# A post-norm transformer layer on one core: in the last batch, who sums the softmax denominators and in which order the last norms, residuals and down products run

## The reference

```python
paths = sigmoid(x @ Wp + bp)                       # 8 heads x depth 5
agree = pq * pk + (1.0 - pq) * (1.0 - pk)
sim = cumprod(agree, axis=-1).sum(axis=-1) / DEPTH
sim = where(triu(k=1), -inf, sim); attn = softmax(sim)
ctx = attn @ (x @ Wv)
x = layernorm(x + ctx @ Wo)
h = silu(x @ wg.T) * (x @ wu.T)                    # hidden 768, int weights / 127
x = layernorm(x + h @ wd.T)
```

## Time and profile before

| | us |
|---|---|
| median of 3 runs | 849.27 (848.09 to 849.35) |
| profiled execution, its own time | 848.94 |
| its span, first to last instruction | 847.1 |
| PE busy | 802.3 (95%) |
| DVE busy | 613.9 (72%) |
| ACT busy | 456.4 (54%) |
| POOL busy | 293.4 (35%) |
| mean granted TensorE clock | 0.991 |

### The profile page before, as it was taken

The page is one execution under the profiler, slowest core; times in us unless marked ns, Lnnn a source line. Parts: engine busy times, 40 slices in busy tenths (PEclk is TensorE's granted clock), DMA queues, the critical chain, the costliest instruction groups (busy, mean ns, idle before and its releaser), DMA issues.

```text
span 847.1 us, 14414 instructions
## 1 busy us (share of the span) xinstructions
PE 802.3 (95%) x5538; PEld 397.6 (47%) x5538; DVE 613.9 (72%) x1101; ACT 456.4 (54%) x721; POOL 293.4 (35%) x266
## 2 busy tenths in 40 slices
PE   6998999999999999999999999999999998999886
PEld 5553364444634455453644536444454444444253
DVE  2767966778667876679666795677766787667966
ACT  1656736556465654657455573655646464465422
POOL 0201522436225262244413462142622425234424
PEclk9999999999999999999999999999999999999998
DMA  7932462042610636006630247105260063400001
GB/s 226 208 105 75 100 160 91 1 103 77 171 50 1 150 83 166 1 6 146 147 102 1 60 91 186 64 1 117 84 150 1 1 150 91 109 1 2 26 0 52
DMA packets 47510, 71.02 MB, mean 84 GB/s; under 512 B 3920, under 2 KB 26704, under 8 KB 47440
## 3 DMA queue, kind: packets, MB, share of 16 engines
q1 hardware_dynamic: 47440, 70.07, 31.7%
HBM read 53.28 MB, written 16.78 MB: 83 GB/s over the span
## 4 chain that ended last, share of the span: by engine, by line
PE 57%; DVE 25%; issue 9%; ACT 5%; POOL 1%; DMA 1%; SPq 0%; DVEq 0%; POOLq 0%; ACTq 0%
PE slot L879 10%; PE misc L960 9%; PE ctx_ps L902 9%; PE misc L853 7%; PE misc L948 7%; PE misc L925 6%; DVE acc L600 5%; PE den_ps L908 5%; DVE work L700 5%; ACT probs L504 4%; DVE x L683 3%; DVE acc L597 3%; DVE x1T_lo L690 2%; PE misc L862 2%; DVE ctx_raw L610 1%
## 5 line engine op out<-in xcount | busy, mean ns | idle before, releaser
L504 ACT ACTIVATE probs<-slot 128x1024 f32<-128x1024 f32 (+3 forms) x384 | 290.2, 808 | 290.4 <-PE slot L879 261.9
L433 POOL TENSOR_SCALAR_AFFINE_SELECT probs<-probs 128x512 f32<-128x512 f32 x128 | 145.9, 1140 | 207.7 <-ACT probs L504 207.5
L447 POOL TENSOR_TENSOR work<-work 128x512 f16<-128x512 f32 x96 | 116.1, 1209 | 177.4 <-ACT work L522 177.4
L902 PE MATMUL ctx_ps<-probs,vz_sb 128*32 128x512 f32 (+3 forms) x1536 | 164.5, 501 | 4.8 <-DVE ctx_raw L610 2.6
L879 PE MATMUL slot<-query_stack,key_stack 128*128 128x512 f16 (+3 forms) x768 | 160.6, 330 | 1.6 <-ACT probs L504 1.0
L948 PE MATMUL misc<-x1T_hi,w_parts 128*128 128x512 f16 x358 | 136.1, 380 | 8.5 <-DVE x1T_lo L690 6.0
L948 PE MATMUL misc<-x1T_lo,w_parts 128*128 128x512 f16 x358 | 135.8, 379 | 0.0
L879 PEld LDWEIGHTS slot<-query_stack,key_stack 128*128 128x128 f16 x768 | 56.6, 98 | 161.6 <-issue 126.2
L600 DVE TENSOR_TENSOR acc<-acc,probs 128x1536 f32<-128x1536 f32 (+3 forms) x64 | 106.5, 1664 | 1.3 <-POOL probs L433 1.1
L700 DVE SCALAR_TENSOR_TENSOR work<-work,misc 128x512 f32<-128x512 f32 x90 | 61.4, 682 | 59.7 <-ACT work L516 59.7
L960 PE MATMUL misc<-w_parts,work 128*128 128x256 bf16 x720 | 84.8, 274 | 2.4 <-POOL work L447 2.0
(11 more groups left out here) (81 smaller groups left out, 738.4 us busy)
## 6 DMA issues: line engine op xcount, KB each, us to landing
key_stack<-phi_dram SPq DMA_DIRECT2D x56, 256.0 KB, 5.8
query_stack<-phi_dram SPq DMA_DIRECT2D x56, 256.0 KB, 6.6
x_sb<-in_x_dram SPq DMA_DIRECT2D x8, 1024.0 KB, 5.3
out_dram<-x SPq DMA_DIRECT2D x15, 512.0 KB, 4.5
xT_sb<-in_xT_dram SPq DMA_DIRECT2D x7, 1024.0 KB, 4.9
phi_dram<-phi_hi SPq DMA_DIRECT2D x14, 256.0 KB, 2.0
phi_dram<-phi_lo SPq DMA_DIRECT2D x14, 256.0 KB, 2.3
key_stack<-phi_dram SPq DMA_DIRECT2D x16, 128.0 KB, 3.1
```

The lines of the kernel that those rows point to most:

```text
L433: pool.affine_select(out=tile, in_=tile, compare_op=ALU.is_ge, fill=0.0, base=0, pattern=[[0, 4], [1, P]], channel_multiplier=-1).then_inc ...
L447: pool.tensor_tensor(hid_lo[:, n % M1, :], hid[:, n % HSLOTS, :], hid_hi[:, n % M1, :], ALU.subtract).then_inc(hid_lo_ready, 1)
L504: act.activation(probs[:, s % P_SLOTS, 2 * p:2 * p + 2, off:CH], slot[p][:, :, off:CH], ACT.Exp).then_inc(slot_drained[p], 1)
L902: mm = pe.matmul(ctx_ps[32 * k:32 * k + 32, off:CH], vz_sb[:, b % 2, j, 32 * h:32 * h + 32], probs[:, s % P_SLOTS, k, off:CH], start=first ...
```

## The change

There are four edits, three of them in the last batch alone.

1. In chunk q = 3 of batch 7, the diagonal steps j = 4 to 7 are no longer added up by VectorE. TensorE multiplies each by ones right behind its `weigh`. `acc` then holds j = 1 to 3 only, and is multiplied by ones behind `weigh` of j = 3 (`SUM_END`). ScalarE's exponentials no longer wait for the sums that are gone.
2. The statistics and the power of the FFN norm of half 0 move ahead in the list, from behind slice 11 to behind slice 6. The rows are still applied behind slice 11.
3. Of the last half, the statistics of both banks come first, then both applications and stores.
4. In `down`, everywhere, the loop over the two tiles goes inside the loop over slices and parts. Each bank now gets start and stop once, and the second bank's matmuls carry the waits for `hid_lo` too.

```diff
--- before.py
+++ after.py
@@ -48,6 +48,12 @@
     ADD_FROM = {2: 3, 3: 1}
     ADDED = [i for i, (q, c, g, j) in enumerate(STEPS) if q in ADD_FROM and j >= ADD_FROM[q]]
     ADDS = [i for i in ADDED if STEPS[i][3] > ADD_FROM[STEPS[i][0]]]
+
+    SUM_END = {(b, q): max(i for i in ADDED if STEPS[i][0] == q and not (b == B - 1 and q == NQ - 1 and i in DIAG))
+               for b in range(B) for q in ADD_FROM}
+
+    def added(b, i):
+        return i in ADDED and i <= SUM_END[b, STEPS[i][0]]
     NA = len(ADD_FROM)
     LAST = {q: max(i for i, s in enumerate(STEPS) if s[0] == q) for q in range(NQ)}
     GROUP_END = {g: max(i for i, s in enumerate(STEPS) if s[2] == g) + 1 for g in range(NG)}
@@ -121,15 +127,15 @@
     def ending():
 
         b = B - 1
-        return ([("sum", b, NS - 1), ("weigh", b, NS - 3)] + gate_pair(b, 2) + [("weigh", b, NS - 2), ("weigh", b, NS - 1)] + halves(b, 2)
+        return ([("weigh", b, NS - 3)] + gate_pair(b, 2) + [("weigh", b, NS - 2), ("weigh", b, NS - 1)] + halves(b, 2)
                 + [("normalise", b, NQ - 1)] + gate_pair(b, 3) + halves(b, 3) + gate_pair(b, 4) + halves(b, 4)
                 + project(b, 1) + norm(0, b, 1) + gate_pair(b, 5) + halves(b, 5) + [("apply", 0, b, 1)]
                 + down(b, 0, 0) + turn_x1(b, 1) + down(b, 0, 1)
-                + gate_pair(b, 6) + gate_pair(b, 7) + halves(b, 6) + gate_pair(b, 8) + halves(b, 7)
+                + gate_pair(b, 6) + norm(1, b, 0) + gate_pair(b, 7) + halves(b, 6) + gate_pair(b, 8) + halves(b, 7)
                 + gate_pair(b, 9) + halves(b, 8) + gate_pair(b, 10) + halves(b, 9) + gate_pair(b, 11) + halves(b, 10)
-                + halves(b, 11) + norm(1, b, 0) + [("apply", 1, b, 0), ("store", b, 0)]
-                + [step for s in range(2) for step in down(b, 1, s)
-                   + [("stats_half", b, 1, s), ("apply_half", b, 1, s), ("store_half", b, 1, s)]])
+                + halves(b, 11) + [("apply", 1, b, 0), ("store", b, 0)]
+                + [step for s in range(2) for step in down(b, 1, s) + [("stats_half", b, 1, s)]]
+                + [step for s in range(2) for step in [("apply_half", b, 1, s), ("store_half", b, 1, s)]])
 
     def between(b, i):
         found = []
@@ -171,7 +177,7 @@
             plan += [("scores", b, i), ("exps", b, i)]
             if i in DIAG:
                 plan += [("mask", b, i)]
-        if s >= 1 and (s - 1) % NS in ADDS and s <= B * NS:
+        if s >= 1 and (s - 1) % NS in ADDS and added(*divmod(s - 1, NS)):
             plan += [("sum", *divmod(s - 1, NS))]
         plan += between(b, i)
         if LAG <= s < B * NS - 1:
@@ -495,7 +501,7 @@
                 if s >= P_SLOTS:
                     act.wait_ge(pv_done, s - P_SLOTS + 1)
                     b2, i2 = divmod(s - P_SLOTS, NS)
-                    if i2 in ADDED:
+                    if added(b2, i2):
 
                         i2 += i2 not in ADDS
                         act.wait_ge(summed, len(ADDS) * b2 + ADDS.index(i2) + 1)
@@ -901,17 +907,17 @@
                     h = 4 * g + k
                     mm = pe.matmul(ctx_ps[32 * k:32 * k + 32, off:CH], vz_sb[:, b % 2, j, 32 * h:32 * h + 32],
                                    probs[:, s % P_SLOTS, k, off:CH], start=first, stop=final)
-                if i not in ADDED:
+                if not added(b, i):
                     if first and NQ * b + q >= 1:
                         pe.wait_ge(den_out, NQ * b + q)
                     for k in range(4):
                         mm = pe.matmul(den_ps[32 * k:32 * k + 32, off:CH], ones[:, :],
                                        probs[:, s % P_SLOTS, k, off:CH], start=first, stop=final)
                 mm.then_inc(pv_done, 1)
-                if i in ADDED and final:
+                if added(b, i) and i == SUM_END[b, q]:
                     pe.wait_ge(summed, len(ADDS) * b + ADDS.index(i) + 1)
                     for k in range(4):
-                        mm = pe.matmul(den_ps[32 * k:32 * k + 32, :], ones[:, :], acc[:, k, :], start=False, stop=True)
+                        mm = pe.matmul(den_ps[32 * k:32 * k + 32, :], ones[:, :], acc[:, k, :], start=False, stop=final)
                     mm.then_inc(acc_used, 1)
 
             def project(b, c, s):
@@ -951,16 +957,18 @@
 
             def down(b, c, s, parts):
                 k = claim("down", b, c, s)
-                for t in (2 * s, 2 * s + 1):
-                    terms = [(a, e, m) for e in range(parts) for m in range(M1) for a in (hid_hi, hid_lo)]
-                    for at, (a, e, m) in enumerate(terms):
-                        if t == 0 and e == 0 and a is hid_hi:
-
-                            pe.wait_ge(hid_lo_ready, GATES * b + M1 * c + m + 1)
+
+                terms = [(a, e, m) for e in range(parts) for m in range(M1) for a in (hid_hi, hid_lo)]
+                for at, (a, e, m) in enumerate(terms):
+                    if e == 0 and a is hid_hi:
+
+                        pe.wait_ge(hid_lo_ready, GATES * b + M1 * c + m + 1)
+                    for t in (2 * s, 2 * s + 1):
                         mm = pe.matmul(misc[k][:, (t % 2) * D:(t % 2 + 1) * D],
                                        a[:, m, t * P:(t + 1) * P],
                                        w_parts[:, 2, e, m * D:(m + 1) * D],
-                                       start=(at == 0), stop=(at == len(terms) - 1))
+                                       start=(at == 0 and t == 2 * s),
+                                       stop=(at == len(terms) - 1 and t == 2 * s + 1))
                 mm.then_inc(misc_filled[k], 1)
 
             def walk(plan, parts=None):
```

## The result

| | before | with the change |
|---|---|---|
| median us | 849.19 (848.09 to 849.35, 6 runs) | 842.46 (842.06 to 845.30, 6 runs) |
| ratio to before | | 0.9933, interval 0.9919 to 0.9947 |
| profiled execution: its own time / span | 848.94 / 847.1 | 842.06 / 840.2 |
| mean granted clock | 0.991 | 0.996 |

The interval leaves no doubt that the kernel is faster, by 4.5 to 6.9 us; the forecast as a ratio, 844.4 / 849.27 = 0.9943, lies inside it. In the profiled execution the 6.9 us between the spans split by six stages of the last batch. They end at these events of the timeline: the `weigh` of j = 3, the gate behind the last chunk, the gate of slice 6, the last residual, the end of the last application, the end of the span.

The account below looks back on a forecast made before the run. PE, busy 95%, was taken as the bound, with time won at its last-batch waits and low clock. Terms -1.2, -1.1, -1.1, -1.7, +0.4 and +0.2 sum to -4.5 us: 848.94 to 844.4, range 842.0 to 847.0.

Parts of the forecast that it names:

- Edit 1: Last chunk's diagonal steps: 2.20 us idle time and 1.7 us low clock go, PE pays 2.7; balance -1.2 us.
- The 1.7 us of low clock in the sum: Diagonal steps of the last chunk: PE's lost time at 1.2 GHz behind the mask wait, claimed as a gain.
- Edit 4, first product: Batch 7's first down product: ten fewer matmuls behind the last `hid_lo`, at 0.11 us each; -1.1 us.
- The fall of the clock stays: First down product of batch 7: PE still idle for 2.9 us, so no clock gain; 1.7 more if none fell.
- rival 2: First down product of batch 7: the clock does not fall there either; 842.7 us, chance 0.15.
- The last product: Batch 7's last down product: -1.1 us from the loops, -1.7 from the clock staying up, +0.4 from early statistics.
- Rival 1: End of batch 7: the clock falls as before; 846.1 us, chance 0.15.
- Edit 2's cost: Early statistics: slice 11 late on DVE and last `hid_lo` slower, +0.2 each; +0.4 us, out of 0 to 1.2.
- Edit 3: End of batch 7: power held beside the application and stores meeting, each bounded 0 to +0.7; +0.2 us for both.
- Rival 4: All batches: down products get slower through held weight loads or alternating bank halves; 853.2 us, chance 0.05.
- Rival 3: Diagonal steps: masks stay slow or something else delays j = 5, costing 0.7 us; 846.3 us, chance 0.10.
- rival 5: Diagonal steps and end clocks give nothing, early statistics and late applications cost their upper ends; 848 us, chance 0.05.

Follow-up runs that it names:

- e1: Kernel before plus only TensorE's products by ones for diagonal steps j = 4 to 7 of the last chunk; 846.52 us, ratio 0.9984.
- e7: Changed kernel, but VectorE adds up the last chunk's diagonal steps again; 844.15 us, ratio 0.9949 to before.
- e2: Kernel before plus only the new loop order of `down` (slices outside, the two tiles inside); 845.96 us, ratio 0.9980.
- e3: Changed kernel, but the application of the first bank stands ahead of the last residual again; 843.62 us, ratio 0.9953 to before.
- e4: Changed kernel, but the statistics of half 0 stand behind slice 11 again; 843.05 us, ratio 0.9944 to before.
- e9: Changed kernel without the early statistics of half 0 and without both applications last; 845.31 us, ratio 0.9954 to before.
- e5: The changed kernel itself, timed once more; 842.90 us, ratio 0.9938 to before.
- e6: Changed kernel, but `down` has tiles outside and slices inside again; 845.76 us, ratio 0.9974 to before.
- e10: Changed kernel with both banks of the last batch's first down product interleaved, slices 0 to 4 ahead of the wait; 840.51 us, ratio 0.9903 to before.
- e8: Changed kernel with both banks interleaved in both last-batch down products, and half 0's statistics ahead of slice 6; 839.70 us, ratio 0.9899 to before.

## Why the prediction was right, and which step failed

**The profile's reading** held: the three waits and what stood behind them are where the time went, and 6.4 of the 6.9 us are in stages that the edits touch. The sum fell short of the trace by 2.4 us: 1.7 for the clock in the first down product, 0.6 for edit 1 and 0.5 ahead of all stages, less 0.4 that the end cost more. What the reading passed over twice is VectorE: it was ready within half a microsecond of PE in the diagonal steps and at the last residual.

**Edit 1** was mis-sized, -1.76 instead of -1.2. The four products by ones cost 0.97 + 0.76 + 0.43 + 0.34 = 2.5 us from start to next start, not 2.7, and the scores of j = 6 took 0.54 instead of 0.82, as before their second half waited for exponentials. The masks were fast as forecast, and e1 and e7 show the 1.8 us with and without the other edits. The 1.7 us of low clock in the sum are not a price that stands by itself: e2, where the clock held, is only 0.35 us shorter in this stretch, because PE then waits for VectorE's last sum. Against e2 edit 1 gives 10.97 - 9.56 = 1.4 us. What edit 1 takes away is the chain of slow masks and sums, with the waits and the low clock inside it.

**Edit 4, first product.** "10 x 0.11 = 1.1" was right: e2 against before 1.10. The step that failed is the next sentence, "The fall of the clock stays: PE is idle for 2.9 us". The idle time was 2.80, and the clock stayed at 1.00; that is the 1.7 us of rival 2. The prediction gave rival 2 a chance of 0.15. But the rival's reason, a shorter idle time, is not shown either. With idle times of 2.80 to 2.89 the clock fell in five traces (e2, e3, e4, e7, e9) and held in two (the change, e5). Two stretches of the same length, of e3 and of e5, with the wait ahead of each:

```profile
811.06 0.92 PE L967 MATMUL slot<-w_parts,work 128*128 128x256 bf16 x4 [2.80 <-POOL work L453]
```

```profile
811.00:817.00 6.00, 5.94 (x38) 5.09 (x39) 2.42 (x5) 1.19 (x2) 0.01 (x1) 0.72 0.01 3
```

```profile
812.14 0.61 PE L967 MATMUL slot<-w_parts,work 128*128 128x256 bf16 x4 [2.81 <-POOL work L453]
```

```profile
812.00:816.00 4.00, 3.86 (x36) 3.56 (x37) 2.27 (x4) 1.08 (x2) 0.09 (x1) 1.00 0.00 0
```

The wait is 2.80 and 2.81, and the clock behind it 0.72 and 1.00. What decides between them stays open. That this term came out as a gain in the profiled execution is luck. The sum should have carried it as a chance over both values instead of a "stays". A fall costs 1.4 to 1.7 us by the stages (19.12 in e9 to 19.45 in e2 and e7, against 17.73), which may be part of the spread of the runs (842.06 to 845.30); not all of it, as the run of 844.88 had a mean granted clock of 0.997 and that of 842.06 one of 0.996.

**The last product** came out at -2.44 against -2.4, but the sum gave the parts to the wrong edits. It booked 1.1 for edit 4 and 1.7 for the clock, and only +0.4 for edit 2. e1, e2 and e9 show that the clock and the loops, alone or together, move the last residual by 0.13 or 0.14 us (19.77 to 19.64 or 19.63), for DVE's chain bounds it. Before the change PE's bank was full at 836.90 + 3.98 = 840.88 and DVE was through with the first application at 840.13 + 0.73 = 840.86, and I took PE alone for the bound. These rows are:

```profile
836.90 3.98 PE L960 MATMUL slot<-w_parts,work 128*128 128x256 bf16 x24
...
840.13 0.73 DVE L676 TENSOR_SCALAR x<-x,mv,rstd 128x256 f32<-128x256 f32 x2 [0.81 <-POOL rstd L443]
```
Edits 2 and 3 shorten DVE's chain; with them and without edit 4 it is 18.42, with edit 4 added 17.33. The sentence that without edit 2 "the earlier PE would have been lost on DVE" was right and should have entered the sum. Rival 1 did not come: the clock held in every one of these ends but that of before. But my reason, an idle time shorter than 1.74 us, is not shown. In e1 the clock held behind 0.70 and 1.25 us of idle time, where before it fell behind 0.71 and 1.25, and in e6 it held behind 0.98 and 1.09. So the -2.4 agrees in part by luck.

**Edit 2's cost** of +0.4: the last `hid_lo` let PE go on 14.06 us behind the gate of slice 6, against 13.74 before, +0.32. The application beside it took 2.56 us instead of 1.38 and delayed nothing.

**Edit 3** forecast at +0.2 with both stores: the power beside the application took 0.80 instead of 0.70 (+0.10 in the chain), and the end behind the last application 3.14 instead of 2.62. So it cost 0.6 us, three times the 0.2. The store rows of the change and of e3 (SP's issues: size, median us to landing):

```profile
out_dram<-x SPq DMA_DIRECT2D x2, 256.0 KB, 2.8
```

```profile
out_dram<-x SPq DMA_DIRECT2D x2, 256.0 KB, 2.1
```

Without edit 3 this stage is 2.61 to 2.67 in five traces; with it, 3.14, 3.31, 3.70 and 3.27 in four and 2.62, 2.68 and 2.72 in three. The lost time stands in one row, SP's own row of the second store. Both stores of the change, then of e4, from SP's timeline (start, us):

```profile
836.09 1.90 SPq L382 DMA_DIRECT2D out_dram<-x  x2
```

```profile
839.71 1.37 SPq L382 DMA_DIRECT2D out_dram<-x  x2
```

In both the second store is issued 1.01 us behind the first. Its row alone takes 0.89 us in the change and 0.37 in e4, e6 and all five traces without edit 3; it takes 1.05 in e5, 1.46 in e7, 1.02 in e10 and 0.46 in e8. The excess over 0.37 is about that of the stage over 2.6. So closeness of the stores is not enough: in e4, e6 and e8 they are as close and lose 0.1 us or nothing, and why they differ is open. Against that edit 3 lets the last residual start 0.87 us earlier (e3).

**Rival 4** is out: the 28 banks of the seven other batches take 2.78 or 2.79 us in e2 as before. **Rival 3** is out by the masks, and rival 5 (848) by the time.

## What to carry to other kernels

When PE and VectorE reach a step within 0.1 us of each other, a gain on one alone is worth about that much; sum an edit's gain only after writing down when the other engine is ready, and test pairs of edits, not edits alone. The same holds for the price of a low clock: it is the full 1.4 to 1.7 us only where nothing but PE bounds the stretch, and was 0.35 us where VectorE's sums stood behind it. Inner loops are best ordered so that what depends on the last operand is last for all outputs, not for one: here ten matmuls behind a wait became idle-time filler, and thirty with both banks interleaved. A sum on VectorE that slows GpSimd's work beside it can cost more than the matmuls that it spares, in the one place where TensorE is idle.

## What the runs showed of the hardware that was not expected

- The granted clock fell behind an idle time of 2.80 us in e3 and not in e5, with the same instructions up to there. Behind 2.20 us it fell before and in e7 and held in e2. Behind two idle times with 1.96 us in sum it fell before; it held behind 1.95 in e1 and 2.07 in e6. The length of the idle time alone does not decide it.
- Three masks of 512 elements a partition took 5.38 us beside VectorE's sums of two SBUF inputs and 1.91 us without. A rule of the Trainium skill, SBUF — State Buffer, "Who interferes with whom", says that such a VectorE instruction and a GpSimd instruction that reads SBUF contend for shared ports, and that this is an exclusive lock. That fits the masks: the one that ran beside the sum of j = 3 ended at 788.43 + 1.93 = 790.36, 0.50 us behind the sum. For the last power beside an application of two rows (its only tensor input is `x`) no blocking for a whole row was seen: it took 0.80 us instead of 0.70.
- The second of two stores of 256 KB issued 1.0 us apart had a row of 0.89 to 1.46 us on SP in four of seven traces, 0.46 in one and 0.37 in two; issued 3.5 to 3.6 us apart it had 0.37 in all five.
